# First feed-forward of a two-layer transformer: VectorE joins the tile two behind first in a step, and on routed steps lowers before it chooses

## The chip, the cores and the metric

The kernel runs on one core of one Trainium2 chip. Its time is the device time of one launch in microseconds (us); smaller is better.

## What is computed

The input is 4 sequences of 512 tokens, each a row of 256 numbers. Four blocks follow one another, each with a residual and a layer norm. The change touches the second, a feed-forward with routing:

```
logits = x @ router_w + router_b                    # 8 experts
p, i   = top_2(softmax(logits)); p = p / sum(p)     # gates: 2 of 8 are not zero
h      = gelu(x @ expert_w[e] + expert_b[e])        # e = 0..7, 256 wide each
x      = layernorm(x + (sum_e gate[e] * h[e]) @ out_w + out_b)
```

All experts are computed for all tokens, and the gates weight them. The first block (attention, 16 heads of 16) ends with its own projection, residual and layer norm, and these are done in the same loop as the feed-forward. The third block (attention with 16 heads of 128) and the fourth (a second feed-forward with routing) come after it and are not changed.

## The kernel before

**Splitting.** Matmuls run in bf16 with each operand in a high part and a low part: `mm3` issues three matmuls (lines 437, 438 and 439). Whatever PE is to multiply by has first to be turned (transposed by PE into a bank, L628), then copied to its high part by ScalarE (`turned_high`, L927), and then VectorE subtracts that high part from the bank to give the low part (`turned_low`, L1206). Only then may PE use it.

**Tiles and steps.** The 2048 tokens are 16 tiles of 128. The loop over `STEPS` is a software pipeline. Step n holds, for different tiles:

- tile n: the eight experts in four matmul groups `experts(n, 0..3)` of two experts each, Gelu by ScalarE after each (L1054), weighting and adding up of experts 0 to 4 by VectorE (`mix(n, 0..2)`, L1436 and L1439), experts 5 to 7 by POOL (L1757, L1762);
- tile n-1 ("behind"): `join_halves` adds POOL's sum to VectorE's (L1445), PE turns the sum ("cm"), `turned_low("cm")` gives its low part, `second_project` multiplies by `out_w`;
- tile n-2: `joined(n-2, 2)` adds the projection to the residual (L1332) and takes the statistics (L1334, L1335), POOL works out the inverse deviation (L1771, L1773), `norm(n-2, 2)` (L1341) finishes the layer norm, PE turns the result ("x2");
- tile n+6 ("ahead"): the same end of the first block: `first_project`, `joined(ahead, 1)`, `norm(ahead, 1)`; tile n+5 is turned as "x1", tile n+7 as "cc", and `context(n+8)` (L1318) makes the operand of the turn "cc" that comes in the next step.

Pieces for tiles past 15 fall away: no "ahead" from step 10 on, no "x1" from step 11 on. Steps 16 and 17 only finish, and the third block's first projections begin in them.

**Routing.** Steps 3, 7 and 11 are routed: PE makes the logits of four tiles, `route` (L1356, L1163, L1164) prepares them, ScalarE takes the exponential with two loads of its function table (L985, L1054), `choose_first` is nine small VectorE instructions (L1193 to L1197), `choose_second` and `gate` are eleven more (L1182 to L1376).

**Order.** Each engine runs its own list in program order, and semaphores tie the lists together. PE's list in a step is: turn x1, `experts(n, 0)`, [logits], `first_project`, `experts(n, 1)`, turn cc, `experts(n, 2)`, turn cm, `experts(n, 3)`, turn x2, `second_project(n-1)`. On a routed step `first_project` follows `experts(n, 1)`. VectorE's list is that of the loop below. ScalarE's list has the Gelus and the high parts in PE's order.

Of the kernel before, what the change touches and what calls it, by code (L numbers as in the profile page):

```python
# [17 lines left out]
NT = NB * TT  # L18
# [138 lines left out]
def build(nc, x_tok_d, x_t_d, wqkv_d, wall_d, const_d, bp_d, outb_d, b2_d, rb_d, eb_d, rw0_d, rw1_d, b1_d, out_d):  # L157
    ctx = ExitStack()
    with ctx:
# [6 lines left out]
        def ds(start, size):  # L166
            return slice(start, start + size)
# [135 lines left out]
        def hold(eng, semaphore, value):  # L303

            if value > 0:
                eng.wait_ge(semaphore, value)
# [22 lines left out]
        def turn_bank(i):  # L329
            return 7 if i < LONE_TURNS else i % 2  # L330
# [873 lines left out]
        def _(dve):  # L1204
            def low(out, bank_cols, hi):
                return dve.tensor_tensor(out, bank_cols, hi, ALU.subtract)  # L1206
# [89 lines left out]
            def kt(ap):  # L1296
                return ap.rearrange("p (k t) -> p k t", k=KE)

            def turned_low(kind, t):
                i = TURNS.index((kind, t))  # L1300
                dve.wait_ge(m["thi"], i + 1)
                if kind == "x2":
                    hi, lo = xt_hi[:, :, t * P:(t + 1) * P], xt_lo[:, :, t * P:(t + 1) * P]
                else:
                    his, los = {"cc": (ta_hi, ta_lo), "cm": (tc_hi, tc_lo), "x1": (tb_hi, tb_lo)}[kind]
                    slot = t % (TB if kind == "x1" else 2)
                    hi, lo = kt(his[slot]), kt(los[slot])
                low(lo, kt(bank[turn_bank(i)][:, 0:E]), hi).then_inc(m["tlo"], 1)
# [14 lines left out]
            def joined(t, which):  # L1323

                rows = x_tok[:, t * E:(t + 1) * E]
                slot = 2 * (which - 1) + t % 2
                dve.wait_ge(m[f"o{which}"], t + 1)
                if which == 1 and t % TT == 0:
                    dve.wait_ge(xb_done, t // TT + 1)
                if which == 2:  # L1330
                    dve.wait_ge(m["xb"], t + 1)
                dve.tensor_tensor(rows, bank[2 if which == 1 else 3][:, 0:E], rows, ALU.add).then_inc(m[f"r{which}"], 1)  # L1332
                dve.wait_ge(m[f"r{which}"], t + 1)
                chain(dve.bn_stats(stats[:, slot, :], rows))  # L1334
                dve.bn_aggr(mv[:, slot, :], stats[:, slot, :]).then_inc(m[f"agg{which}"], 1)  # L1335

            def norm(t, which):
                rows = x_tok[:, t * E:(t + 1) * E]
                slot = 2 * (which - 1) + t % 2
                dve.wait_ge(m[f"rstd{which}"], t + 1)  # L1340
                dve.tensor_scalar(rows, rows, mv[:, slot, 0:1], rstd[:, slot:slot + 1], ALU.subtract, ALU.mult  # L1341
                                  ).then_inc(m[f"x{which}"], 1)

            def sums_inverse(half):

                heads = slice(half * NH // 2, (half + 1) * NH // 2)
                dve.wait_ge(a["vc"], (half + 1) * NT // 2)
                dve.reciprocal(rcc[:, heads, :], ctx0[:, heads, :, D0:VC].rearrange("p h q d -> p h (q d)")
                               ).then_inc(m["rc"], 1)
                dve.wait_ge(m["rc"], half + 1)  # L1350

            def route(b):

                dve.wait_ge(m["lg"], b + 1)
                tiles_b = slice(b * TT, (b + 1) * TT)
                dve.tensor_tensor(lg[:, tiles_b, :], bank[2][:, 0:TT * NX].rearrange("p (t x) -> p t x", x=NX),  # L1356
                                  rb_bc[:, :].unsqueeze(1).to_broadcast([P, TT, NX]), ALU.add).then_inc(m["lgc"], 1)
                dve.wait_ge(m["lgc"], b + 1)
                router_max(dve, chain, lg[:, tiles_b, :], TT, m["lgd"])

            def choose_first(b):
                router_first(dve, chain, TT, m["ex"], b + 1)

            def choose_second(b):
                router_second(dve, chain, TT)
# [57 lines left out]
            def mix(t, p):  # L1423

                dve.wait_ge(m["ge"], 4 * t + p + 1)
                if p == 0:

                    if t >= 2:
                        dve.wait_ge(m["tp"], TURNS.index(("cm", t - 2)) + 1)
                    if t % TT == 0:  # L1430
                        dve.wait_ge(m["gates"], t // TT + 1)
                for x in range(2 * p, min(2 * p + 2, DVE_X)):
                    part = ge[p][:, (x % 2) * E:(x % 2 + 1) * E]
                    gate = gates[:, t, x:x + 1]
                    if x == 0:
                        ins = dve.tensor_scalar(comb[t % 2], part, gate, None, ALU.mult)  # L1436
                    else:
                        dve.wait_ge(m["mul"], DVE_X * t + x)
                        ins = dve.scalar_tensor_tensor(comb[t % 2], part, gate, comb[t % 2], ALU.mult, ALU.add)  # L1439
                    ins.then_inc(m["mul"], 1)  # L1440

            def join_halves(t):
                dve.wait_ge(m["psum"], (NX - DVE_X - 1) * (t + 1))
                dve.wait_ge(m["mul"], DVE_X * (t + 1))
                dve.tensor_tensor(comb[t % 2], comb[t % 2], pc[t % 2], ALU.add).then_inc(m["join"], 1)  # L1445

            def l1_low(which, g, j=0):
                half = (g % 2) * TOK
                if which == "q":
                    hold(dve, c["phi"], 4 * g + j + 1)  # L1450
                    low(qt_lo[j % 2], bank[4][:, :], qt_hi[j % 2]).then_inc(c["plo"], 1)
                elif which == "k":
                    hold(dve, c["kvh"], 2 * g + 1)
                    low(k1_lo[:, ds(half, TOK)], bank[5][:, :], k1_hi[:, ds(half, TOK)]
                        ).then_inc(c["kvl"], 1)
                else:
                    hold(dve, c["kvh"], 2 * g + 2)
                    low(v1_lo[:, ds(half, TOK)], bank[5][:, :], v1_hi[:, ds(half, TOK)]
                        ).then_inc(c["kvl"], 1)

            for n in STEPS[len(EARLY):]:
                here, ahead, behind = 0 <= n < NT, n + LEAD + 1, n - 1
                if 0 <= n + LEAD < NT:
                    turned_low("x1", n + LEAD)
                if n == EARLY[-1] + 1:
                    sums_inverse(1)
                if n == NT:
                    l1_low("k", 0)
                routed = 0 <= n + 4 < NT and (n + 4) % TT == TT - 1
                if routed:  # L1470
                    route((n + 4) // TT)
                if here:
                    mix(n, 0)
                if 0 <= n - 2:
                    joined(n - 2, 2)
                if 0 <= behind < NT:
                    join_halves(behind)
                if 0 <= ahead < NT:
                    joined(ahead, 1)
                if 0 <= n + LEAD + 2 < NT:  # L1480
                    turned_low("cc", n + LEAD + 2)
                if n == NT:
                    l1_low("q", 0, 0)
                if here:
                    mix(n, 1)
                if 0 <= n - 2:
                    norm(n - 2, 2)
                if 0 <= ahead < NT:
                    norm(ahead, 1)
                if routed:  # L1490
                    choose_first((n + 4) // TT)
                if 0 <= behind < NT:
                    turned_low("cm", behind)
                if n == NT:
                    l1_low("v", 0)
                if here:
                    mix(n, 2)
                if routed:
                    choose_second((n + 4) // TT)
                    gate((n + 4) // TT)  # L1500
                if 0 <= n + LEAD + 3 < NT:
                    context(n + LEAD + 3)
                if 0 <= n - 2:
                    turned_low("x2", n - 2)
# [76 lines left out]
            for b, i, what in TAIL:  # L1581
                if what == "hidden":
                    n = NF * b + i
# [293 lines left out]
```

## Time and profile before

| what | us |
|---|---|
| median of 3 runs | 946.39 (946.23 to 951.05) |
| the profiled execution | 945.18 |
| its span, first to last instruction | 943.4 |
| PE busy in the span | 855.9 (91%) |
| VectorE (DVE) busy | 703.5 (75%) |
| ScalarE (ACT) busy | 515.3 (55%) |
| POOL busy | 389.9 (41%) |

The changed loop lies between about 257 us (the first Gelu of step 0) and 412 us (the first scores of the third block). The first Gelu of a step marks its start well: steps 4, 5 and 6 start at 294.00, 302.91 and 311.82, so such a step lasts 8.91 us. Routed step 7 starts at 320.73 and step 8 at 335.11, 14.38 us later; step 3 lasts 13.21 and step 11 lasts 10.80. Steps 10 and 12 to 15, with nothing "ahead", last 7.18. In the rows, the number in brackets is idle time of the engine before the instruction, with the instruction that ended it.

### The profile page before, as it was taken

What the parts mean: (1) busy time and instruction counts of PE and PEld (TensorE: products, weight loads), DVE (VectorE), ACT (ScalarE), POOL (GpSimd) and SP (SyncE); (2) the same over time, 40 slices, a digit from 0 to 9 for tenths busy, and PEclk for the clock granted to TensorE, in tenths of its full rate; (3) what the DMA queues carried; (4) which work ended last, traced back from release to release, by engine and by line L of the source; (5) the groups of instructions that cost most, each with busy time, mean ns of one, the idle gap of its engine ahead of it and who ended that gap; (6) DMA issues with size and microseconds to landing.
All of it is one profiled execution on the core that took longest, in us unless ns stands there. A gap on an engine that the chain in (4) does not pass through costs nothing.

```text
span 943.4 us, 22476 instructions
## 1 busy us (share of the span) xinstructions
PE 855.9 (91%) x8350; PEld 539.2 (57%) x8457; DVE 703.5 (75%) x1953; ACT 515.3 (55%) x1201; POOL 389.9 (41%) x731
## 2 busy tenths in 40 slices
PE   5899999986698798979999999999999999899986
PEld 2455555553354444445656767677766666586654
DVE  3677777785678877669998888888888888523566
ACT  3477677764443534456676555555565555423542
POOL 4455466534265644523433323333333333200275
PEclk7899999999899989999999999999999999999999
DMA  7333332310000000016677555556556555400011
GB/s 264 102 92 91 70 79 63 84 24 6 2 1 1 1 1 1 1 28 126 122 117 124 101 97 95 104 98 102 100 99 103 103 97 103 86 2 1 1 46 45
DMA packets 210428, 65.64 MB, mean 70 GB/s; under 512 B 203008, under 2 KB 206608, under 8 KB 210192
## 3 DMA queue, kind: packets, MB, share of 16 engines
q1 hardware_dynamic: 210320, 64.19, 34.5%
q8 instruction: 68, 1.11, 0.5%
q14 instruction: 40, 0.33, 0.1%
HBM read 17.92 MB, written 4.19 MB: 23 GB/s over the span
## 4 chain that ended last, share of the span: by engine, by line
PE 63%; DVE 11%; issue 10%; POOL 8%; DMA 4%; ACT 3%; SPq 1%; POOLq 0%; DVEq 0%; ACTq 0%
PE bank L438 14%; PE bank L439 13%; PE bank L437 12%; PE bank L564 4%; PE bank L792 3%; PE bank L794 3%; PE bank L793 3%; DVE nm L1264 3%; DMA att<-w_lo 3%; PE bank L511 2%; PE bank L506 2%; POOL scr L1757 2%; POOL scr L1762 2%; PE bank L487 2%; DVE w_lo L1288 2%
## 5 line engine op out<-in xcount | busy, mean ns | idle before, releaser
L1022 ACT ACTIVATE att<-att,nm 128x512 f32<-128x512 f32 (+3 forms) x256 | 141.4, 553 | 104.5 <-DVE nm L1277 103.1
L437 PE MATMUL bank<-w_hi,scr 128*128 128x256 bf16 (+1 forms) x567 | 169.9, 300 | 13.3 <-DVE scr L1206 12.4
L438 PE MATMUL bank<-w_lo,scr 128*128 128x256 bf16 (+1 forms) x574 | 172.5, 301 | 0.7 <-issue 0.2
L439 PE MATMUL bank<-w_hi,scr 128*128 128x256 bf16 (+1 forms) x572 | 171.7, 300 | 0.1
L927 ACT ACTIVATE scr<-bank 128x256 bf16<-128x256 f32 (+3 forms) x208 | 110.4, 549 | 96.5 <-PE bank L794 40.4
L1264 DVE TENSOR_REDUCE nm<-bank 128x1 f32<-128x512 f32 (+3 forms) x256 | 110.6, 484 | 40.6 <-PE bank L511 40.5
L1277 DVE CUSTOM_DVE_ANT_0 att<-bank,consts 128x512 f32<-128x512 f32 (+3 forms) x256 | 113.4, 483 | 15.7 <-PE bank L439 15.7
L1806 POOL TENSOR_SCALAR wqkv_hi<-att,rr 128x512 bf16<-128x512 f32 (+3 forms) x128 | 66.0, 537 | 138.2 <-DVE rr L1294 138.2
L973 ACT ACTIVATE att<-bank 128x512 f32<-128x512 f32 (+1 forms) x192 | 90.7, 527 | 51.8 <-PE bank L548 51.4
L1206 DVE TENSOR_TENSOR scr<-bank,scr 128x256 bf16<-128x256 f32 (+1 forms) x144 | 76.0, 538 | 49.4 <-ACT scr L927 49.2
L1806 POOL TENSOR_SCALAR w_hi<-att,rr 128x512 bf16<-128x512 f32 (+3 forms) x128 | 66.0, 536 | 106.4 <-DVE rr L1294 106.4
L792 PE MATMUL bank<-att,w_hi 128*128 128x384 bf16 (+2 forms) x320 | 84.5, 274 | 7.7 <-DMA att<-w_lo 7.1
L438 PE MATMUL bank<-xt_lo,w_hi 128*128 128x512 bf16 x224 | 85.4, 381 | 3.1 <-issue 0.2
L793 PE MATMUL bank<-att,w_hi 128*128 128x384 bf16 (+2 forms) x320 | 87.6, 274 | 0.0
L439 PE MATMUL bank<-xt_hi,w_lo 128*128 128x512 bf16 x223 | 85.0, 381 | 0.0
L794 PE MATMUL bank<-att,w_lo 128*128 128x384 bf16 (+2 forms) x320 | 84.4, 274 | 0.0
L437 PEld LDWEIGHTS bank<-w_hi,scr 128*128 128x128 bf16 x576 | 56.9, 99 | 39.3 <-DVE scr L1206 18.0
L438 PE MATMUL bank<-w_lo,w_hi 128*128 128x512 bf16 (+3 forms) x256 | 76.6, 299 | 0.6 <-DVE w_lo L1206 0.6
L1054 ACT ACTIVATE scr<-bank 128x512 f32<-128x512 f32 x64 | 38.2, 598 | 63.8 <-PE bank L439 36.4
L437 PE MATMUL bank<-w_hi 128*128 128x512 bf16 (+1 forms) x255 | 73.0, 299 | 0.0
L439 PE MATMUL bank<-w_hi,w_lo 128*128 128x384 bf16 (+1 forms) x255 | 72.9, 299 | 0.0
L1206 DVE TENSOR_TENSOR w_lo<-bank,w_hi 128x512 bf16<-128x512 f32 x96 | 66.4, 692 | 7.3 <-ACT w_hi L927 6.7
(180 smaller groups left out, 2026.7 us busy)
## 6 DMA issues: line engine op xcount, KB each, us to landing
scr<-wall_in SPq DMA_DIRECT2D x19, 512.0 KB, 4.9
x_tok<-x_tok_in SPq DMA_DIRECT2D x1, 2048.0 KB, 9.6
v_by_token<-scr SPq DMA_DIRECT2D x16, 128.0 KB, 1.8
scr<-v_by_token SPq DMA_DIRECT2D x16, 128.0 KB, 3.3
scr<-x_t_in SPq DMA_DIRECT2D x3, 512.0 KB, 5.8
out<-x_tok SPq DMA_DIRECT2D x3, 512.0 KB, 2.7
scr<-wqkv_in SPq DMA_DIRECT2D x2, 384.0 KB, 3.6
att<-w_hi SPq DMA_TRANSPOSE x32, 3.3
```

Source lines behind the costliest of these rows:

```text
L437: pe.matmul(out, l_hi, r_hi, start=start, stop=False, skip_group_check=check)
L438: pe.matmul(out, l_hi, r_lo, start=False, stop=False, skip_group_check=check)
L439: return pe.matmul(out, l_lo, r_hi, start=False, stop=stop, skip_group_check=check)
L792: pe.matmul(out, v1_hi[:, vs], hi, start=(kt, q0) == (0, 0), stop=False, skip_group_check=True)
L793: pe.matmul(out, v1_hi[:, vs], lo, start=False, stop=False, skip_group_check=True)
L794: last = pe.matmul(out, v1_lo[:, vs], hi, start=False, stop=(kt == TT - 1), skip_group_check=True)
L927: return act.activation(out, in_, ACT.Copy)
L1022: last = act.activation(at, at, ACT.Exp, bias=nm[:, j % 2, qt:qt + 1], scale=-1.0, accum_out=rs[:, j % 2, qt:qt + 1])
L1206: return dve.tensor_tensor(out, bank_cols, hi, ALU.subtract)
L1264: last = dve.tensor_reduce(nm0[:, p % 2, h, qt:qt + 1], bank[n % 2][:, col:col + w], AX.X, ALU.max)
L1277: last = dve.tensor_tensor_reduce(s_sb[j % 2][:, S_OFF[qt]:S_OFF[qt] + w], bank[turn][:, col:col + w], mask[:, 512 - w:512], -scale, HUGE, ...
L1806: pool.tensor_scalar(ps_hi[j % 2][:, at], s_sb[j % 2][:, at], rr[:, j % 2, qt:qt + 1], 1.0, ALU.mult, ALU.mult).then_inc(c["row"], 1)
```

## The change

Two moves in VectorE's list, no instruction added or taken away. `joined(n-2, 2)` goes from behind `mix(n, 0)` to the front of the step, ahead of `route` and `mix(n, 0)`. On routed steps `turned_low("cm", n-1)` goes ahead of `choose_first`.

```
                 if n == NT:
                     l1_low("k", 0)
+                if 0 <= n - 2:
+                    joined(n - 2, 2)
                 routed = 0 <= n + 4 < NT and (n + 4) % TT == TT - 1
                 if routed:
                     route((n + 4) // TT)
                 if here:
                     mix(n, 0)
-                if 0 <= n - 2:
-                    joined(n - 2, 2)
                 if 0 <= behind < NT:
                     join_halves(behind)
...
                 if 0 <= ahead < NT:
                     norm(ahead, 1)
+                if 0 <= behind < NT:
+                    turned_low("cm", behind)
                 if routed:
                     choose_first((n + 4) // TT)
-                if 0 <= behind < NT:
-                    turned_low("cm", behind)
```

## Rows read from the trace of the kernel before

**Rows 1.** Two stretches: length, PE, PEld, DVE, ACT, POOL busy, clock, DMA.

```profile
321.00:335.00 14.00, 10.67 (x63) 5.36 (x61) 11.56 (x42) 6.13 (x11) 5.69 (x11) 0.78 0.00 1
...
360.00:371.00 11.00, 8.06 (x62) 3.85 (x60) 8.90 (x35) 5.94 (x10) 4.65 (x8) 1.00 0.01 1
```

**Rows 2.** Waits from 250 to 410 us: total, times, longest.

```profile
PE bank L437 <- DVE scr L1206: 10.1, 10, 2.8
```

**Rows 3.** Timeline of PE, step 5: last expert matmul, turn x2, second_project.

```profile
307.35 0.38 PE L438 MATMUL bank<-w_lo,scr 128*128 128x512 bf16 x1
307.56 0.38 PE L439 MATMUL bank<-w_hi,scr 128*128 128x512 bf16 x1
308.36 0.44 PE L628 MATMUL bank<-consts,x_tok 128*128 128x128 f32 x2 [0.42 <-DVE x_tok L1341]
309.10 0.28 PE L437 MATMUL bank<-w_hi,scr 128*128 128x256 bf16 x1 [0.30 <-DVE scr L1206]
```

**Rows 4.** Timeline of VectorE, step 5.

```profile
303.54 0.35 DVE L1436 TENSOR_SCALAR scr<-scr,att 128x256 f32<-128x256 f32 x1 [1.43 <-ACT scr L1054]
...
304.33 0.42 DVE L1332 TENSOR_TENSOR x_tok<-bank,x_tok 128x256 f32<-128x256 f32 x1
...
305.67 0.42 DVE L1332 TENSOR_TENSOR x_tok<-bank,x_tok 128x256 f32<-128x256 f32 x1
...
306.68 0.39 DVE L1206 TENSOR_TENSOR scr<-bank,scr 128x256 bf16<-128x256 f32 x1
...
308.64 0.40 DVE L1206 TENSOR_TENSOR scr<-bank,scr 128x256 bf16<-128x256 f32 x1
```

**Rows 5.** Timeline of ScalarE: high part of cc in step 5.

```profile
305.44 0.38 ACT L927 ACTIVATE scr<-bank 128x256 bf16<-128x256 f32 x1
```

**Rows 6.** Timeline of POOL: deviation for the tile ahead in step 5.

```profile
307.13 0.74 POOL L1773 TENSOR_TENSOR rstd<-var_e,neg_half 128x1 f32<-128x1 f32 x1
```

**Rows 7.** Timeline of VectorE, routed step 7 and the start of step 8.

```profile
321.41 0.19 DVE L1356 TENSOR_TENSOR lg_sb<-bank,rb_bc 128x32 f32<-128x32 f32 x1 [1.47 <-PE bank L439]
...
325.09 0.42 DVE L1206 TENSOR_TENSOR scr<-bank,scr 128x256 bf16<-128x256 f32 x1
...
327.08 0.17 DVE L1193 TENSOR_REDUCE r1c<-att 128x4 f32<-128x32 f32 x1
...
329.58 0.42 DVE L1206 TENSOR_TENSOR scr<-bank,scr 128x256 bf16<-128x256 f32 x1
...
335.74 0.35 DVE L1436 TENSOR_SCALAR scr<-scr,att 128x256 f32<-128x256 f32 x1 [1.84 <-ACT scr L1054]
```

**Rows 8.** Timeline of PE: second_project at the end of routed steps 7 and 11.

```profile
330.06 0.40 PE L437 MATMUL bank<-w_hi,scr 128*128 128x256 bf16 x1 [2.82 <-DVE scr L1206]
...
368.22 0.28 PE L437 MATMUL bank<-w_hi,scr 128*128 128x256 bf16 x1 [2.30 <-DVE scr L1206]
```

**Rows 9.** Timeline of ScalarE: high part of cc in step 7.

```profile
324.68 0.38 ACT L927 ACTIVATE scr<-bank 128x256 bf16<-128x256 f32 x1
```

**Rows 10.** Timeline of VectorE: the start of step 4, behind routed step 3.

```profile
294.63 0.35 DVE L1436 TENSOR_SCALAR scr<-scr,att 128x256 f32<-128x256 f32 x1 [0.67 <-ACT scr L1054]
```

**Rows 11.** Timeline of VectorE: mix(12, 0), behind routed step 11.

```profile
371.35 0.35 DVE L1436 TENSOR_SCALAR scr<-scr,att 128x256 f32<-128x256 f32 x1
```

**Rows 12.** Timeline of PE, step 9: last expert matmul, second_project.

```profile
348.45 0.38 PE L439 MATMUL bank<-w_hi,scr 128*128 128x512 bf16 x1
...
350.02 0.28 PE L437 MATMUL bank<-w_hi,scr 128*128 128x256 bf16 x1 [0.43 <-DVE scr L1206]
```

**Rows 13.** PE in step 14: end of experts(14, 2), turn cm, experts(14, 3).

```profile
387.33 0.38 PE L439 MATMUL bank<-w_hi,scr 128*128 128x512 bf16 x1
387.96 0.44 PE L628 MATMUL bank<-consts,scr 128*128 128x128 f32 x2 [0.25 <-DVE scr L1445]
388.24 0.38 PE L437 MATMUL bank<-w_hi,scr 128*128 128x512 bf16 x1
```

More of the change, by code:

```diff
@@ L1468, in _ @@
                     l1_low("k", 0)
+                if 0 <= n - 2:
+                    joined(n - 2, 2)
                 routed = 0 <= n + 4 < NT and (n + 4) % TT == TT - 1
@@ L1473, in _ @@
                     mix(n, 0)
-                if 0 <= n - 2:
-                    joined(n - 2, 2)
                 if 0 <= behind < NT:
@@ L1489, in _ @@
                     norm(ahead, 1)
+                if 0 <= behind < NT:
+                    turned_low("cm", behind)
                 if routed:
                     choose_first((n + 4) // TT)
-                if 0 <= behind < NT:
-                    turned_low("cm", behind)
                 if n == NT:
```

## The prediction, made before the changed kernel was run

> **What bounds the kernel now.** The page says that PE is busy for 91% of the span, so the first question is where it is not. Several of the slices that the page shows below 9 tenths lie in the loop of the change. The view of stretches, with one stretch for each step, then shows which steps they are. Two of its rows [rows 1] are to be read together: in the 14 us of routed step 7 PE is busy for 10.67 and VectorE for 11.56, with TensorE's granted clock at 0.78 of full; in routed step 11 it is 8.06 of 11, at a clock of 1.00. The waits name the cause: PE stands longest before the first matmul of `second_project` (L437), for the low part that VectorE makes on L1206, 10.1 us in ten waits with the longest of 2.8 [rows 2].
>
> The timeline shows the pattern. In an ordinary step the last expert matmul starts at 307.56. Matmuls of that size start 0.22 apart (307.35 to 307.56), so PE is free at 307.78, but it turns x2 at 308.36 because `norm(n-2, 2)` is late, and starts `second_project` at 309.10 because the low part of cm is late [rows 3]. Without waits it would start at 307.78 plus 0.22 for the turn, 308.00. PE loses 1.10 of its 8.91 us. VectorE meanwhile stood idle for 1.43 us before `mix(5, 0)`, waiting for a Gelu, and then worked without a gap until that low part [rows 4]. The loop closes through PE: a late `second_project` makes the next step's first Gelu late, and with it the next `mix`. So a step is as long as VectorE's chain from `mix(n, 0)` to the low part of cm, plus PE's way from there to the next Gelu. What shortens this chain shortens the step.
>
> **First move, ordinary steps (2, 5, 6).** Nothing is added or removed: three instructions, L1332, L1334 and L1335, leave the chain. They take 1.01 from start to start (305.67 to 306.68, the same three for the tile ahead; 304.33 is where they stand now) [rows 4]. They go into the idle 1.43 before `mix`. Their operand is there: `second_project(n-2)` ran in the step before, ahead of the turn x1 whose low part VectorE makes first in the step. So `mix(n, 0)` keeps its start, and 0.42 of idle is left. No DMA and no queue of SP is moved past. Behind the join on VectorE now wait `route` and `mix(n, 0)`; ScalarE's Gelus and PE's banks wait for the mix only a step later.
>
> What is late next: with 1.01 taken out, the low part of cc could start at 305.67, but its high part is done by ScalarE only at 305.44 + 0.38 = 305.82 [rows 5]. It starts at 305.86 instead of 306.68, 0.82 earlier. From its start to `second_project` it is 309.10 - 306.68 = 2.42 without a gap [rows 3, 4], so `second_project` starts at 308.28 instead of 309.10. POOL doesn't hold it: the deviation of the tile ahead, ready at 307.87 [rows 6], moves by the full 1.01, to 306.86, and `norm(n-2, 2)` runs before it. PE could start at 308.00, so VectorE, by 0.28, is still the one waited for. Gain 0.82 in each of three steps: 2.46.
>
> **Step 9** has no cc, so nothing of ScalarE's holds the chain. PE is free at 348.45 + 0.22 + 0.22 = 348.89, and `second_project` started at 350.02 [rows 12]. VectorE's chain is 1.01 shorter, and the last 0.12 comes from a wait of the second norm for POOL that shrinks: PE is the bound, gain 1.13. If only the join counts, 1.01.
>
> **Steps 10 and 13 to 15** have no tile ahead. Here the join delays `join_halves`, and PE waits for it before the turn cm: 387.33 + 0.22 = 387.55 against 387.96, and the turn then takes 0.28 to the next matmul instead of 0.22 [rows 13]. The wait goes away, 0.47 in each, and nothing else of PE's waits in these steps: 4 x 0.47 = 1.88.
>
> **Routed steps 3, 7, 11, first move.** VectorE is idle for 1.47 before `route`, waiting for PE's logits [rows 7]; the join fits in. But the low part of cc at 325.09 is held by ScalarE, which loads two function tables around the exponential and gives the high part at 324.68 + 0.38 = 325.06 [rows 7, 9]. The join's 1.01 becomes idle time just before it. Gain within the routed step: 0.
>
> **Routed steps, second move.** `choose_first` runs from 327.08 to 329.58, 2.50 us, ahead of the low part of cm [rows 7]. Now that low part starts at 327.08 and `second_project` at about 327.55, not 330.06 [rows 8]. Its high part was made before 326, and no engine waits for the choices, since the gates come after them on VectorE in any case. But VectorE's own list isn't shorter: the choices, the gates, `context` and the low parts end when they ended before. PE runs ahead by 2.5 and then stands before the turn cc of step 8, which needs `context`, and before turns cm and x2. What is won is VectorE's idle time that PE's lateness caused: 1.84 before `mix(8, 0)` [rows 7], 0.67 before `mix(4, 0)` [rows 10], none before `mix(12, 0)` [rows 11]. The join, now ahead of that mix, fills that same time, so the two moves share it: from the front join on, VectorE works without a gap up to the low part of cm. Gain 1.84 + 0.67 + 0 = 2.51 for three pairs of a routed step and the next (3-4, 7-8, 11-12). The first move alone would get 0.67 and 1.01 of it.
>
> Steps 0 and 1 have no tile two behind, and in steps 16 and 17 the join is first already: 0. The blocks after the loop start earlier and are the same.
>
> **The clock.** In the stretch of step 7 the granted clock was 0.78, part of it at 1.2 GHz of its 2.4, behind a standstill of 2.82; step 11 had one of 2.30 and no fall, clock 1.00 [rows 1, 8]. Both standstills shrink to about that of an ordinary step, but in their place PE stands three times in steps 4, 8 and 12, by my reckoning some 3.5 us in sum in each of steps 4 and 8: it comes 2.5 early, and a VectorE without gaps leaves it about 1 more to wait. I take no cost: PE waits for VectorE there, and slower matmuls fill these waits. The bound above: a fall of the same depth (0.22 of 14 us, 3.1) behind each of three routed steps, if it reaches into steps in which PE is the bound; the bound below: 0.
>
> The Trainium skill (TensorE: Matmul & The Clock Gate, What's actually happening) says that the gate passes half or all of the pulses by how busy PE has been recently. This trace agrees that the clock fell behind the longest standstill; by the page alone several shorter ones could have the same effect, and then the sum would be that of the second rival below.
>
> **Sum.** 2.46 + 1.13 + 1.88 + 2.51 = 7.98, say 8.0 us. The profiled execution, 945.18 with a span of 943.4, becomes 937.2, its span 935.4. The median of before is 946.39, 1.2 above that execution; from it, 938.4 us.
>
> **Rivals.**
> 1. *The forecast*, 938.4, its own range 936.5 to 940.5. Chance 0.72. Upward of the sum: 0.28 more in each of three ordinary steps if ScalarE's copy comes earlier, 0.8. Downward: a few tenths in each step if VectorE's instructions get slower beside POOL's work with which they now meet; at 0.1 in each of 14 steps, 1.4.
> 2. *The clock falls in steps 4, 8 and 12* and stays low into PE-bound work. For it: PE's idle time there is spread and more in sum than before. Against: the clock kept 1.00 in step 11 with 2.30 in one piece. Price: up to 3 x 3.1 = 9.3, less the part that waits hide; taking a third to two thirds, 3 to 6 us back, 941.5 to 944.5, say 943. Chance 0.13.
> 3. *The routed steps give nothing*, because something else holds the step behind them (POOL's weighting, or PE's turn cc waiting for `context`). For it: VectorE's list there is as long as before. Against: the idle time of 1.84 and 0.67 has the Gelu as its only cause. Then 8.0 - 2.5 = 5.5, 940.9. Chance 0.10.
> 4. *Slower: the front join blocks VectorE.* In the new place it waits for `second_project(n-2)` with `route` and all mixes behind it. If that product came later than VectorE gets there by more than the 0.42 left, every us beyond it goes into the step. It needs over 8.0/14 = 0.57 beyond the slack in each of 14 steps to cancel the gain, and 0.57 + 4.7/14 = 0.9 to be slower by 0.5%; at 1.2 beyond it the time is 946.4 + 8.8 = 955. Against: PE's order puts the product ahead of the turn x1 that VectorE has by then already lowered, and in steps without x1 its six short matmuls begin right behind the turn x2. Chance 0.02.
> That the change does nothing (VectorE waits for the same Gelu and PE for the same low part) would need the idle 1.43 to be no idle time; 946.4, chance 0.03.
>
> **Range and chances.** Two in ten may be left out: the forecast's range widened to cover rival 3 and the near end of 2 gives 936.2 to 941.5. A difference of 0.5%, 4.7 us, is about what a measurement of this kernel can tell. Faster by more (below 941.7): rivals 1 and 3 and a tenth of 2, less a little for their own tails, 0.82. Within: the rest of 2, the case of nothing and the tails, 0.15. Slower: 0.03.
>
> **What would show it.** In the changed profile, ordinary steps last 8.09 instead of 8.91, with the joins' L1332 before `mix(n, 0)` and hardly any idle time there; PE's wait before L437 falls from 0.30 to under 0.1 more than the turn's own tail, and that before the turn x2 disappears. Step 10 and steps 13 to 15 last about 6.7 (7.18 before) without a wait on L1445. In the routed steps `second_project` starts straight behind the turn x2, the wait of 2.8 is gone, and new PE waits stand in steps 4 and 8, for `context`, L1445 and L1341. Wrong would be: a granted clock under 0.9 in those steps, VectorE idle before the first L1332 of a step for a matmul, or idle time left before `mix(4, 0)` and `mix(8, 0)`.

## The result, and the profile after

The changed kernel takes 941.08 us (median of 12 runs, 936.23 to 945.83); the kernel before, 12 runs beside it, 949.48 (945.43 to 953.85). The ratio is 0.9918, with a 95% interval of 0.9896 to 0.9940: 7.8 us less, between 5.7 and 9.9. The prediction said 8.0 less and 938.4; that base, 946.39 from three runs, lay 3.1 below the median of twelve. The measured time lies near the upper end of the range of 936.2 to 941.5, and above the forecast's own 936.5 to 940.5. Two later comparisons of the same kernel gave 0.9920 (0.9889 to 0.9951) and 0.9949 (0.9923 to 0.9976).

The profiled execution took 939.53, span 937.7 against 943.4. The steps, from the starts of their first Gelus ("to third block" ends with the first exponential of the third block; a "pair" is a routed step and the next; a hundredth more or less is rounding):

| us | before | forecast | after |
|---|---|---|---|
| steps 2, 5, 6, each | 8.91 | 8.09 | 8.12 |
| pair 3-4 | 22.12 | 21.45 | 21.71 |
| pair 7-8 | 23.29 | 21.45 | 21.71 |
| step 9 | 8.72 | 7.59 | 7.72 |
| pair 11-12 | 17.98 | 17.98 | 18.00 |
| steps 10, 13, 14, each | 7.18 | 6.71 | 6.70 |
| step 15 to third block | 20.68 | 20.21 | 20.14 |
| the loop, step 0 to third block | 155.94 | 147.96 | 148.62 |

The loop is 7.3 us shorter. The third block, whose code is the same, takes 400.2 us in this execution and 398.5 in that of before, which hides 1.7 of it in the spans.

PE's wait before `second_project` was 10.1 us in the waits of before, with a longest of 2.8 [rows 2]. Now, in the waits of the changed kernel over 240 to 410 us:

```profile
PE bank L437 <- DVE scr L1206: 1.9, 7, 0.4
```

An ordinary step, on VectorE (the same step 5 as in [rows 4]):

```profile
300.83 0.41 DVE L1332 TENSOR_TENSOR x_tok<-bank,x_tok 128x256 f32<-128x256 f32 x1
...
302.33 0.35 DVE L1436 TENSOR_SCALAR scr<-scr,att 128x256 f32<-128x256 f32 x1 [0.42 <-ACT scr L1054]
...
304.65 0.42 DVE L1206 TENSOR_TENSOR scr<-bank,scr 128x256 bf16<-128x256 f32 x1
...
306.64 0.41 DVE L1206 TENSOR_TENSOR scr<-bank,scr 128x256 bf16<-128x256 f32 x1
```

The join stands ahead of the mix, the idle time before the mix is 0.42 as worked out, and the low part of cm follows 4.31 behind the mix instead of 5.10. On PE the wait before the turn x2 is gone, and the one before `second_project` is a third of a microsecond (it could start at 306.79) [rows 3]:

```profile
306.36 0.38 PE L439 MATMUL bank<-w_hi,scr 128*128 128x512 bf16 x1
306.57 0.38 PE L628 MATMUL bank<-consts,x_tok 128*128 128x128 f32 x2
307.10 0.28 PE L437 MATMUL bank<-w_hi,scr 128*128 128x256 bf16 x1
```

Routed step 7 and the next, on VectorE: low part of cc, the two norms, low part of cm, choices, join, mix.

```profile
322.30 0.42 DVE L1206 TENSOR_TENSOR scr<-bank,scr 128x256 bf16<-128x256 f32 x1 [0.61 <-ACT scr L927]
...
323.66 1.30 DVE L1341 TENSOR_SCALAR x_tok<-x_tok,mv,rstd 128x256 f32<-128x256 f32 x2
324.88 0.41 DVE L1206 TENSOR_TENSOR scr<-bank,scr 128x256 bf16<-128x256 f32 x1
325.21 0.17 DVE L1193 TENSOR_REDUCE r1c<-att 128x4 f32<-128x32 f32 x1
...
326.07 0.19 DVE L1183 TENSOR_TENSOR att<-att,r1c 128x32 f32<-128x32 f32 x1
326.30 0.64 DVE L1184 TENSOR_TENSOR att<-att,consts 128x32 f32<-128x32 f32 x1
...
331.35 0.42 DVE L1332 TENSOR_TENSOR x_tok<-bank,x_tok 128x256 f32<-128x256 f32 x1
...
332.38 0.35 DVE L1436 TENSOR_SCALAR scr<-scr,att 128x256 f32<-128x256 f32 x1
```

The idle 1.84 of [rows 7] is gone and nothing waits from 322.30 on. The standstill of 2.82 [rows 8] has become four shorter ones on PE, before `second_project` and, in step 8, before the turns cc, cm and x2 (the wait before the turn x2 of step 7 itself grew from 0.44 to 0.95):

```profile
325.34 0.28 PE L437 MATMUL bank<-w_hi,scr 128*128 128x256 bf16 x1 [0.38 <-DVE scr L1206]
...
331.25 0.41 PE L628 MATMUL bank<-consts,scr 128*128 128x128 f32 x2 [1.19 <-DVE xt_lo L1206]
333.64 0.44 PE L628 MATMUL bank<-consts,scr 128*128 128x128 f32 x2 [0.68 <-DVE scr L1445]
336.20 0.44 PE L628 MATMUL bank<-consts,x_tok 128*128 128x128 f32 x2 [0.82 <-DVE x_tok L1341]
```

The stretches of steps 7 and 8 (columns as in [rows 1]) show the clock at 1.00 throughout, where it was 0.78 over step 7:

```profile
318.00:328.00 10.00, 8.67 (x73) 4.83 (x70) 8.20 (x26) 6.34 (x11) 5.71 (x11) 1.00 0.00 0
328.00:340.00 12.00, 9.01 (x57) 4.58 (x54) 10.56 (x36) 4.26 (x9) 5.85 (x11) 1.00 0.01 3
```

### The profile page after: what moved, and what is told of

Read it like the earlier page. It is cut to its first block, busy times and chain, and to the rows that moved or that the text cites. A ratio compares the mean times of both kernels' runs of the same rounds, so it can differ in the third digit from the quotient of the medians.

```text
span 937.7 us, 22580 instructions
## 1 busy us (share of the span) xinstructions
PE 859.6 (92%) x8457; PEld 537.5 (57%) x8457; DVE 705.5 (75%) x1953; ACT 514.7 (55%) x1201; POOL 386.8 (41%) x731
## 4 chain that ended last, share of the span: by engine, by line
PE 66%; DVE 16%; DMA 6%; issue 5%; ACT 4%; POOL 2%; SPq 1%; POOLq 0%; DVEq 0%; ACTq 0%
PE bank L437 14%; PE bank L439 13%; PE bank L438 13%; DMA att<-w_lo 5%; PE bank L564 4%; PE bank L792 3%; PE bank L794 3%; PE bank L793 3%; DVE nm L1264 3%; DVE w_lo L1288 2%; PE bank L511 2%; PE bank L506 2%; PE bank L487 2%; DVE att L1277 1%; ACT scr L927 1%
## 5 line engine op out<-in xcount | busy, mean ns | idle before, releaser
L437 PE MATMUL bank<-xt_hi,w_hi 128*128 128x512 bf16 x224 | 85.5, 382 | 0.8 <-ACT scr L1137 0.8
L437 PE MATMUL bank<-w_hi 128*128 128x512 bf16 (+3 forms) x256 | 73.6, 300 | 0.4 <-DVE w_lo L1206 0.4
L439 PE MATMUL bank<-w_hi,w_lo 128*128 128x512 bf16 (+3 forms) x256 | 73.3, 299 | 0.0
```

Source lines behind the costliest of these rows:

```text
L437: pe.matmul(out, l_hi, r_hi, start=start, stop=False, skip_group_check=check)
L439: return pe.matmul(out, l_lo, r_hi, start=False, stop=stop, skip_group_check=check)
```

## The experiments

In what follows a ratio is always to runs of the kernel before on the same chip. The steps are read as in the table above.

**One move at a time.** `e1_front_join_alone` has only the join's move, `e2_low_part_alone` only that of the low part:

```
e1:                                    e2:
+ if 0 <= n - 2: joined(n - 2, 2)        if 0 <= ahead < NT: norm(ahead, 1)
  routed = ...                         + if 0 <= behind < NT: turned_low("cm", behind)
  if routed: route(...)                  if routed: choose_first(...)
  if here: mix(n, 0)                   - if 0 <= behind < NT: turned_low("cm", behind)
- if 0 <= n - 2: joined(n - 2, 2)
```

> The join of the tile two behind stands first in the step; the low part of cm stays behind the first choices, as before. My theory (VectorE's chain from the mix to the low part of cm sets the step; the join fills its idle time): ordinary steps 5 and 6 last 8.12 as in the changed kernel, step 9 lasts 7.73, steps 10 and 13 to 15 last 6.70. In the pairs of a routed step and the next only part of the idle time before mix(4, 0) and mix(8, 0) is filled: pair 3-4 gains 0.4 to 0.75, pair 7-8 gains 0.7 to 1.0, PE's wait of about 2.8 before second_project on routed steps is back. The loop gains 6.2 to 6.8 us of the changed kernel's 7.3. Rival (both moves are needed, since the standstill of 2.8 us sets the clock and the pace behind it): pairs 3-4 and 7-8 gain nothing and the loop gains 5.2 or less.

Measured: 947.82, ratio 0.9976 (0.9953 to 0.9999), only 2.3 us. Steps 5 and 6 last 8.12, step 9 lasts 7.72, steps 10, 13 and 14 last 6.70, as expected. Of the pairs, 7-8 takes 22.29 (before 23.29), also as expected, but 3-4 takes 23.27 (before 22.12) and 11-12 takes 20.60 (before 17.98), so that the loop gains 2.0 us and not 6.2 to 6.8. Neither theory said that a pair would get longer. The timeline of PE in step 3 shows why: behind the standstill of 2.76 matmuls of 512 columns start 0.43 apart, at 1.2 GHz, where they start 0.22 apart at 2.4. The granted clock over the step is 0.81, as the stretch below that (a row of the windows) shows. The clock fell behind the standstills of steps 7 and 11 (2.75 and 2.84) too.

```profile
291.42 0.44 PE L628 MATMUL bank<-consts,x_tok 128*128 128x128 f32 x2 [0.94 <-DVE x_tok L1341]
294.62 0.39 PE L437 MATMUL bank<-w_hi,scr 128*128 128x256 bf16 x1 [2.76 <-DVE scr L1206]
...
296.30 0.63 PE L437 MATMUL bank<-w_hi,scr 128*128 128x512 bf16 x1
296.72 0.63 PE L438 MATMUL bank<-w_lo,scr 128*128 128x512 bf16 x1
```

```profile
284.00:299.00 15.00, 11.30 (x76) 5.70 (x74) 12.76 (x45) 6.40 (x11) 6.59 (x13) 0.81 0.00 1
```

> The low part of cm goes ahead of the first choices on the three routed steps; the join stays behind the mix. My theory: ordinary steps stay at 8.91 and steps 10 and 13 to 15 at 7.18; only VectorE's idle time before mix(4, 0) and mix(8, 0) is won, 0.67 and 1.84 (up to 0.08 more each), pair 11-12 gains 0. The loop gains 2.5 us, the two moves alone add up to more than both together (about 9 against 7.3), because they fill the same idle time. Rival (the standstill's length counts): each routed step gains about the 2.3 to 2.8 us by which second_project comes earlier, 7 to 8 us in sum.

Measured: 949.54, ratio 1.0004 (0.9982 to 1.0026), no gain in the time. The loop of its profile is 154.17, 1.8 less than before, with pairs of 21.83, 21.83 and 18.40, and 7.53 instead of 7.18 in step 13. From step 3 to step 13 that is only 1.0 less; 1.5 comes from behind step 15 (19.18 instead of 20.68), where PE stood for 3.24 as before but the clock did not fall this time, and step 0 was 0.7 longer. The moves don't overlap, as I had said they would. They add up to more together (7.8) than alone (2.3 and nothing). That is the wrong way round for my account of the routed steps, in which they share VectorE's idle time.

`e3_changed_again` is the changed kernel again, to see what repeats.

> The changed kernel once more, unaltered, to tell the loop from what comes after it. My theory: the loop's steps repeat to 0.05 us (8.12; 21.7 for a routed pair; 6.70), and what differs between executions, several us, lies behind the loop, in the third block, where PE waits for transposing DMAs. Rival: the steps behind routed steps vary between executions, with the clock.

Measured: 941.33, ratio 0.9920 (0.9889 to 0.9951). All steps repeat within 0.02: 8.12; 21.72 and 21.73; 18.01; 6.70. The clock didn't fall in them, so the rival had nothing to show here. The third block took 398.7 us here and 400.2 in the first profile, with the same code.

**The standstill without its clock.** A new theory: `second_project` may be 2.5 us late without any harm, since PE makes it up while VectorE works; what costs is that the clock falls behind the standstill. `e7` and `e8` fill the standstill, the one with e1's order, the other with that of the kernel before, and leave `second_project` where it is:

```
 def second_project(t):
+    if t in (2, 6, 10):
+        hold(pe, m["r2"], t)
+        fill(bank[3][:, :], 10)          # ten matmuls, ones by ones, 512 columns
     pe.wait_ge(m["tlo"], TURNS.index(("cm", t)) + 1)
```

> The front join alone, with ten matmuls on ones by ones, 512 columns each, put into PE's standstill before second_project on the three routed steps (they write the bank that second_project then overwrites, so nothing that is computed changes; 2.2 us). VectorE's order is that of e1. My theory now (the price of the standstill is the clock, not the lateness of second_project): no fall of the clock in steps 3 to 12; pairs 3-4 and 7-8 last 21.4 to 21.7 and pair 11-12 18.0, where e1 had 23.27, 22.29 and 20.60; the loop lasts 148 to 149 as in the changed kernel, the time is within 1 us of the changed kernel's. Rival (the lateness counts): pairs stay above 22, the time stays near that of e1, 2 us below before.

> The kernel before with the same ten matmuls in the standstill, VectorE's order unchanged. My theory: pairs 3-4 and 7-8 last 21.4, as against 22.12 and 23.29, with second_project where it was, as late as before; pair 11-12 stays at 18.0; ordinary steps 8.91. The loop lasts 153.3, and against the kernel before the time falls by 2 to 4 us, more than the loop's 2.6 in the one profile where executions of before have three falls. Rival (the lateness of second_project makes VectorE's idle time): pairs stay over 22, no gain.

Measured: e8 944.5, ratio 0.9960 (0.9939 to 0.9980), with pairs of 21.35, 21.36 and 17.97; the loop takes 154.0. e7 940.15, ratio 0.9913 (0.9881 to 0.9944), with pairs of 21.63, 21.64 and 18.28; the loop takes 148.9. In e8 the matmuls on ones (L647) end at 333.09, `second_project` comes at 333.75, 9.33 behind the start of step 7, just as late as in the kernel before. Two rows of the timeline follow, PE's and then VectorE's; the mix of step 8 has no wait:

```profile
330.77 2.32 PE L647 MATMUL bank<-ones_b 128*128 128x512 bf16 x10
333.75 0.28 PE L437 MATMUL bank<-w_hi,scr 128*128 128x256 bf16 x1 [0.66 <-DVE scr L1214]
```

```profile
337.51 0.35 DVE L1444 TENSOR_SCALAR scr<-scr,att 128x256 f32<-128x256 f32 x1
```

So VectorE's idle time before `mix(4, 0)` and `mix(8, 0)` was made by the clock alone. Without a fall the old order already gives pairs of 21.35, shorter than those of the changed kernel. Filling gives e1 back what it lacked: from 0.9976 to 0.9913, about the ratio of the changed kernel.

**Do the falls come and go?**

> The kernel before, unaltered, once more in a profile. My theory: the steps without a routed one repeat to 0.02 us (8.91, 8.72, 7.18); what may differ is whether the clock falls behind the standstills of 2.8 and 2.3 us: pairs 3-4 and 7-8 between 21.4 (no fall) and 23.3, pair 11-12 between 18.0 and 20.6. Rival: all steps repeat, the falls too.

Measured: 951.48 in one run. Pair 3-4 takes 23.27, pair 7-8 takes 21.33 behind a standstill of 2.81 after which the clock did not fall, and pair 11-12 takes 19.54, because the clock fell behind the 2.30 this time. All other steps repeat. Stretches of steps 3, 7, and 11 with the start of 12 (clock third from the end of the row):

```profile
284.00:297.00 13.00, 9.76 (x78) 5.61 (x76) 10.49 (x36) 6.40 (x11) 8.24 (x14) 0.90 0.01 3
...
324.00:338.00 14.00, 10.35 (x84) 6.08 (x85) 11.48 (x39) 7.14 (x14) 9.33 (x16) 1.00 0.01 2
...
363.00:377.00 14.00, 11.13 (x74) 4.93 (x71) 9.69 (x36) 5.88 (x10) 6.33 (x11) 0.88 0.00 1
```

Pair 7-8 is an experiment that the chip made by itself: the same kernel, the same standstill, no fall, and 21.33 instead of 23.29.

> The low part of cm moved alone, once more in a profile, since its time came out like that of before although its loop was 1.8 us shorter in the one profile. My theory: pairs 3-4 and 7-8 repeat at 21.83; pair 11-12 is 18.4, or up to 2 us more if the clock falls behind the standstill of 3.1 us in step 12. Rival: everything repeats, and the time of before would have to be shorter than in its profile in the other executions.

Measured: 945.54 in one run. The pairs 3-4 and 7-8 repeat at 21.82 and 21.83, and 11-12 takes 20.06 behind a standstill of 3.07 in step 12, after which the clock fell. The loop is 156.55 here and 154.17 in the other profile. Of these 2.4, 1.7 come from that pair and 1.5 from a fall behind step 15, less 0.8 in step 0. Falls like these take up part of what e2 should have gained; the two loops of before are 155.94 and 157.36.

**How much room the join has in its new place.** One more statistics instruction (0.43 us), in the front join (e5), or behind the mix (e6). It writes the same numbers again.

```
e5, joined(), for which == 2, t < 14:      e6, the loop:
  chain(dve.bn_stats(stats[...], rows))      if here:
+ chain(dve.bn_stats(stats[...], rows))          mix(n, 0)
                                           +     if 0 <= n - 2: again(n - 2)
```

> The changed kernel with the statistics of the tile two behind taken twice in the front join (one more 128x256 statistics instruction, 0.43 us, 0.46 from start to start, in steps 2 to 15). My theory: in ordinary steps VectorE has 0.42 of idle time left there, so steps 5 and 6 stay within 0.05 of 8.12 and steps 13 to 15 stay at 6.70; in the routed pairs 3-4 and 7-8, where VectorE works without a gap from the choices to the low part of cm of the next step, the pair grows by 0.46, from 21.72 to about 22.2. Rival (the front join already holds back the mix): ordinary steps grow by the full 0.46.

> The same extra statistics instruction, but behind mix(n, 0), where the join stood before. My theory: it lies on the chain: ordinary steps 5 and 6 grow by 0.46 less the 0.27 that VectorE waits for the high part of cc, to about 8.3; the routed pairs grow by 0.46 at most; steps 13 to 15 stay near 6.70, where PE is the bound with some room. Rival (place makes no difference, VectorE's sum counts): the same steps as with the instruction in the front.

Measured, in one profiled run each (943.68 and 946.77 us): e5 8.12, e6 8.37 to 8.38 in ordinary steps. The first Gelus of steps 5 and 6, e5 and then e6:

```profile
306.12 0.60 ACT L1054 ACTIVATE scr<-bank 128x512 f32<-128x512 f32 x1 [1.25 <-PE bank L675]
...
314.24 0.60 ACT L1054 ACTIVATE scr<-bank 128x512 f32<-128x512 f32 x1 [1.25 <-PE bank L675]
```

```profile
306.47 0.60 ACT L1054 ACTIVATE scr<-bank 128x512 f32<-128x512 f32 x1 [1.25 <-PE bank L675]
...
314.84 0.60 ACT L1054 ACTIVATE scr<-bank 128x512 f32<-128x512 f32 x1 [1.25 <-PE bank L675]
```

The pairs grow to 22.18 in both, by 0.46. This settles place against sum: ahead of the mix the instruction is free in an ordinary step, behind it costs 0.25 (in step 9, which has no cc, all 0.46), and in a routed pair it costs all of itself in either place, for there VectorE works without a gap. Steps 13 and 14 stay at 6.70 in both. In pair 11-12 the clock fell in both (20.15 and 20.13).

**Two attempts to do better.** `e4` puts `mix(n, 1)` ahead of the low part of cc, in the changed kernel:

```
+if here: mix(n, 1)
 if 0 <= n + LEAD + 2 < NT: turned_low("cc", n + LEAD + 2)
-if here: mix(n, 1)
```

> The changed kernel, with mix(n, 1) ahead of the low part of cc in VectorE's list. In the changed kernel VectorE waits 0.1 to 0.6 for that low part's high part, while the Gelu of mix(n, 1) is already done. My theory: ordinary steps go from 8.12 to about 7.95, the routed pairs 3-4 and 7-8 (21.7) lose 0.2 to 0.3 each, the others stay: 0.8 to 1.0 us less in the loop, 0.1% of the time, under what the timing can tell. Rival (ScalarE, not VectorE, now holds the step through its high parts): no step gets shorter; a turn then waits for the later low part of cc, and steps get 0.1 to 0.3 longer.

Measured: 943.69, ratio 0.9932 (0.9904 to 0.9959), not to be told from the changed kernel's. Ordinary steps take 8.01 (0.11 less), pairs 3-4 and 7-8 take 21.49 (0.23 less), step 1, which has no join, takes 8.18 instead of 7.95, and pair 11-12 takes 19.65 with a fall. The pairs gained what was expected, the ordinary steps 0.11 of the expected 0.17.

`e9` combines e7 with that swap from step 2 on, and fills two more standstills: 24 matmuls on ones before step 0, 12 in step 17 before the last turn x2.

> A version built from what the runs showed: the front join, ten matmuls on ones in the standstill of each routed step, mix(n, 1) ahead of the low part of cc from step 2 on, and matmuls on ones in two more standstills, 24 where PE waits 6.0 us before step 0 and 12 where it waits 3.24 us before the last turn x2. Nothing that is computed changes. My theory: no fall of the clock from step 0 to the start of the third block; the first Gelu of step 0 about 1 us earlier than in e7 (258.3), ordinary steps 8.0, pairs 21.4, the way from the first Gelu of step 15 to the third block's first exponential 19 instead of 20.2; the loop about 147. Against the changed kernel 2 to 4 us faster. Rival (the clock's falls before step 0 and behind step 17 are hidden): only the 0.5 us of the swap is won, which the timing can't tell from nothing.

> The changed kernel once more on the same chip as e9, for a fair comparison. Ordinary steps 8.12, pairs 21.72, pair 11-12 18.0 if the clock doesn't fall behind the standstill of 2.7 in step 12 and about 19.7 if it does; the time 0.8% below before.

Measured: e9 938.84, ratio 0.9918 (0.9887 to 0.9948); e10, the changed kernel on the same chip, 941.61, ratio 0.9949 (0.9923 to 0.9976). By these e9 is 2.8 us ahead, but the intervals overlap. Its trace says the same: the loop takes 147.0 against 148.6, the way from step 15 to the third block 18.7 against 20.2. The stretch ahead of step 0 (clock third from the end), e9 and then the changed kernel:

```profile
245.00:257.00 12.00, 10.09 (x60) 5.03 (x57) 8.02 (x33) 3.47 (x6) 1.84 (x4) 1.00 0.00 1
```

```profile
245.00:257.00 12.00, 5.32 (x25) 2.37 (x25) 7.53 (x31) 2.28 (x4) 1.47 (x3) 0.72 0.01 1
```

Its pairs took 21.77 where 21.4 was expected; I have not looked into that.

## Why the prediction was right, and where it was wrong

**Ordinary steps: right.** 0.79 in each of three, for 0.82. The chain of VectorE from the mix to the low part of cm sets them; the join left it and found room. The 0.79 is the chain's own 5.10 less 4.31. e1 gives the same 8.12 alone, and e5 and e6 show the chain from both sides.

**Step 9: size off.** 1.00 for 1.13. Only the join's 1.01 was won, the bound that the prediction named; PE didn't become the bound there: it is free at 344.52 and starts `second_project` at 344.65. The remaining 0.12 should have come from a shorter wait of the second norm, but the two norms take 0.85 to the next instruction before and after.

**Steps 10 and 13 to 15: right.** 0.48 in each, for 0.47; e5 and e6, in which they stay at 6.70, show that VectorE has room there.

**Routed pairs: the sum near, the cause wrong. This is the step that failed.** The term was 2.51 and measured 1.97 in the two profiled executions (0.41, 1.58 and -0.02). It is the step that says "What is won is VectorE's idle time that PE's lateness caused", and with it that the first move alone would get 0.67 and 1.01 of it. For the first of these e1 shows a loss of 1.15; that the second came out (1.00) is luck, since the clock fell there too, only for a shorter time. The lateness caused none of the idle time: 2.5 us late, but at full clock, the first Gelu of step 8 is still done before VectorE has finished its list. I had the numbers for this. From `second_project` to the next first Gelu it was 2.72 in step 5 (309.10 to 311.82) and 5.05 in step 7 (330.06 to 335.11). The difference of 2.3 is more than the idle 1.84. The idle times before the three mixes also go with the clock in the trace of before: 1.84 where it granted 0.72, 0.67 where it granted 0.86, none where it did not fall [rows 7, 10, 11]. Stretches behind the standstills of steps 3 and 7 of the kernel before:

```profile
288.00:300.00 12.00, 9.72 (x47) 4.73 (x48) 10.58 (x37) 3.24 (x8) 4.90 (x10) 0.86 0.00 1
...
326.00:338.00 12.00, 8.69 (x38) 4.25 (x38) 9.40 (x35) 2.47 (x6) 4.33 (x8) 0.72 0.00 1
```

Instead I put the clock among the rivals, as a danger of the new order. It was the price of the old one. e8, e7, and pair 7-8 of e11 show it; e1 shows what the first move is worth while the standstill remains.

It follows that this term of the forecast, and with it the nearness of 7.8 to 8.0, was partly luck. The routed pairs of the kernel before vary with the clock (3-4 and 7-8: 22.12, 23.29, 23.27, 21.33; 11-12: 17.98, 19.54), those of the changed kernel did not in three profiles. Against the other profile of before, the same term would have measured 2.72. The prediction also took the missing fall behind 2.30 as evidence against its rival 2; e11 had a fall there.

**A second term was missed.** The pair without falls is 21.35 in the old order and 21.71 in the new. VectorE lost 0.48 at the two norms, which take 1.22 to the next instruction where they took 0.74. In the changed kernel's timeline these of POOL ran beside them or just before them, and a sum later beside L1184:

```profile
322.86 0.60 POOL L1757 TENSOR_SCALAR scr<-scr,att 128x256 f32<-128x256 f32 x1 [0.26 <-ACT scr L1054]
323.43 0.88 POOL L1779 TENSOR_TENSOR x_tok<-x_tok,outb_bc 128x256 f32<-128x256 f32 x1
...
326.17 0.72 POOL L1762 TENSOR_TENSOR scr<-scr 128x256 f32<-128x256 f32 x1
```

L1184 started at 326.30 and took 0.64 instead of 0.19: it ended at 326.94, right behind POOL's 326.89. The join of the tile ahead comes 0.7 earlier in the step than in the old order, so POOL is done with its deviation earlier and starts its share of the mix while the norms, held by the late low part of cc, are still to come. Line by line, from the low part of cc of step 7 to `mix(8, 0)`, the changed kernel against e8 loses 0.47 at the norms, 0.44 at L1184 and 0.11 at the two L1439 ahead of the norms, and wins back 0.69 at four places where the old order met POOL's work instead (L1195, L1186, L1197 and the L1439 behind the low part of cm). That is nearly all of the 0.36 between 21.35 and 21.71. In e2 the choices meet POOL's work too (timeline of e2, VectorE):

```profile
331.76 0.19 DVE L1182 TENSOR_REDUCE r1c<-att 128x4 f32<-128x32 f32 x1
331.99 0.56 DVE L1183 TENSOR_TENSOR att<-att,r1c 128x32 f32<-128x32 f32 x1
332.58 0.42 DVE L1184 TENSOR_TENSOR att<-att,consts 128x32 f32<-128x32 f32 x1
333.03 0.19 DVE L1185 TENSOR_REDUCE r1c<-att 128x4 f32<-128x32 f32 x1
```

Of these small instructions, those with two operands in SBUF stretch, the reductions with one don't. The Trainium skill (SBUF — State Buffer, Who interferes with whom) says that VectorE and GpSimd share a port pair as an exclusive lock, which a VectorE instruction with two SBUF inputs can meet when the GpSimd one reads SBUF, one in a two-port mode can meet too, and a reduction cannot. These rows agree for the small instructions. The norm has only one tensor as input, and no run here shows in which mode it ran, so for its 0.47 the cause is not shown beyond its coming beside POOL's work. The prediction allowed 0.1 a step for this; it is nothing in ordinary steps and 0.3 to 0.4 in each of the pairs 3-4 and 7-8.

**The rivals.** No front join waited for its product (rival 4). The clock didn't fall in steps 4 and 8 of the changed order in any of its three profiles, though PE stands there for 3.0 us in four pieces (rival 2; the prediction reckoned with 3.5); behind the one piece of 2.7 in step 12 it did not fall in those three, but did in e4, which has it too. Behind 3.16 and 3.14 in e5 and e6 it fell. That leaves a part of rival 2 standing.

**What stays open.** e2's time equals that of before, while its two loops are 1.8 and 0.8 us shorter than those of before in order of length. The falls of the clock in single profiles (in step 0, in step 12 and behind step 15) differ by as much, but how the falls are spread over many executions was not measured. Nor were the differences outside the loop explained: over 14 profiles the first Gelu starts between 256.2 and 262.0 us, and from the first to the last exponential of the third block it is 396.2 to 401.7 us. Ranges of 5.8 and 5.5 us are large enough for most of the spread of some 10 us in the times; that they make it up is not shown.

## What to carry to other kernels

Follow the in-order chain that closes the step, and move what isn't part of it into that engine's idle time; the gain can be read to a tenth of a microsecond, and where ScalarE's or PE's next result caps it too. When an engine seems idle because PE was late, compare PE's pace before and behind its standstill first: if the matmuls behind it are slower, it is the clock that is being paid for, and a few idle matmuls in the standstill test that in one run. Two moves that share a cause can be worth more together than alone, so undo them one by one before giving either the credit.

## What the runs showed of the hardware

- The clock falls behind some standstills of PE and not behind others of the same length, in the same kernel: 2.81 with and without (e11), 2.30 with and without (e11 and [rows 8]), 3.09 without and 3.07 with (e2 and e12). In these traces a fall lasted between three and seven microseconds, beginning in the standstill or up to 1.5 us behind it. The length of the fall sets its price: in the kernel before it is 6.8 us in step 7, with 1.84 of VectorE's idle time behind it, and 3.4 in step 3, with 0.67. The Trainium skill (TensorE: Matmul & The Clock Gate, What's actually happening) says that the point at which the clock rises at a kernel's start varies from run to run; what varies between these profiles is whether it falls, and when.
- Ten matmuls on ones in a standstill of 2.3 to 2.8 us kept the clock at 2.4 GHz in all nine standstills that were filled with them (e7, e8, e9).
